# Value matmuls of the feed-forward units: 512 columns in every second step in place of 256 in every step

## The reference

```python
def ffn(hidden_states, ...):                 # twice, with the same weights
    weights = softmax over the top 2 of 4 experts, from the pooled tokens
    q, k, v = [hidden_states @ (mix of the experts' W) + b]   # B=2, T=1024, H=16, D=8
    scores = einsum('bthd,bshd->bhts', q, k) / sqrt(D)
    attn = softmax(scores, axis=-1)
    out = einsum('bhts,bshd->bthd', attn, v).reshape(B, T, C)
    return out @ Wo + bo
x = x + 0.5 * ffn(layernorm(x))
x = x + causal_attention(layernorm(x))
x = x + 0.5 * ffn(layernorm(x))
```

## Time and profile before

| | |
|---|---|
| median of three executions | 1330.35 us (1326.4 to 1460.52) |
| the profiled execution | 1325.41 us, of which the span from the first to the last instruction is 1323.7 us |
| PE busy in the span | 1180.9 us (89%) |
| DVE busy | 1073.0 us (81%) |
| ACT busy | 918.3 us (69%) |
| POOL busy | 343.3 us (26%) |
| exponentials of the units, line 761 | 1024 of 598 ns |
| row maxima, line 925 | 512 of 1217 ns |
| value matmuls, line 1228 | 3584 records |

### The profile page before, as it was taken

One profiled execution on the slowest core, in us unless ns is written; L12 is line 12 of the kernel. 1 busy time (PEld: TensorE's weight loads), 2 busy tenths in 40 slices (PEclk: granted clock), 3 DMA queues, 4 the chain that ended last, 5 costly groups with the idle time before them and its releaser, 6 DMA issues. The chain is left out here.

```text
span 1323.7 us, 33144 instructions
## 1 busy us (share of the span) xinstructions
PE 1180.9 (89%) x10992; PEld 495.5 (37%) x10992; DVE 1073.0 (81%) x1749; ACT 918.3 (69%) x1943; POOL 343.3 (26%) x777
## 2 busy tenths in 40 slices
PE   4499999999987999999989999997869999999996
PEld 3122222222244555555565555554722222222222
DVE  6899999999986677766736777666489999999996
ACT  3189999988955666666635666665328999998893
POOL 4400000002002455544424555445220000000200
PEclk9689999999997999999999999998968999999998
DMA  4711122443111000000000000000333122244312
GB/s 101 226 43 50 55 64 61 89 85 79 48 45 27 20 20 19 20 19 20 20 19 19 20 20 19 20 18 1 99 92 93 47 58 60 61 89 85 85 41 64
DMA packets 53811, 70.06 MB, mean 53 GB/s; under 512 B 21264, under 2 KB 31440, under 8 KB 53712
## 3 DMA queue, kind: packets, MB, share of 16 engines
q1 hardware_dynamic: 53712, 68.75, 20.9%
HBM read 37.79 MB, written 22.54 MB: 46 GB/s over the span
## 5 line engine op out<-in xcount | busy, mean ns | idle before, releaser
L925 DVE TENSOR_REDUCE neg_max<-ps 128x1 f32<-128x1024 f32 x512 | 591.6, 1217 | 23.2 <-PE ps L1197 21.4
L761 ACT ACTIVATE arena<-ps 128x512 f32<-128x512 f32 x1024 | 545.4, 598 | 83.0 <-PE ps L1212 70.7
L1212 PE MATMUL ps<-arena 50*128 50x512 bf16 x1024 | 322.8, 387 | 15.5 <-ACT arena L761 9.9
L1228 PE MATMUL ps<-arena 128*32 128x256 f32 (+1 forms) x3584 | 315.8, 424 | 8.7 <-ACT arena L761 3.1
L1197 PE MATMUL ps<-arena 48*128 48x512 bf16 x1024 | 297.5, 396 | 14.9 <-DVE neg_max L925 13.9
L1001 DVE TENSOR_REDUCE a_neg_max<-ps 128x1 f32<-128x129 f32 (+7 forms) x256 | 192.9, 753 | 130.8 <-PE ps L1335 130.4
L688 ACT ACTIVATE arena<-ps 128x64 f32<-128x64 f32 (+7 forms) x256 | 104.5, 408 | 172.4 <-PE ps L1349 170.3
L682 ACT ACTIVATE arena<-ps,a_neg_max 128x129 f32<-128x129 f32 (+7 forms) x256 | 189.4, 740 | 33.1 <-DVE a_neg_max L1001 32.0
L1329 PE MATMUL ps<-arena 64*128 64x321 f32 (+7 forms) x512 | 192.1, 456 | 7.6 <-ACT arena L682 5.1
L596 POOL TENSOR_SCALAR arena<-arena,a_rsum 128x128 f32<-128x128 f32 (+7 forms) x256 | 190.7, 745 | 18.3
L1331 PE MATMUL ps<-arena 64*128 64x320 f32 (+7 forms) x512 | 191.9, 456 | 0.0
(11 more groups left out here) (120 smaller groups left out, 920.3 us busy)
## 6 DMA issues: line engine op xcount, KB each, us to landing
arena<-stack_dram SPq DMA_DIRECT2D x128, 192.0 KB, 3.3
stack_dram<-arena SPq DMA_DIRECT2D x48, 256.0 KB, 3.7
o_dram<-arena SPq DMA_DIRECT2D x32, 256.0 KB, 2.1
arena<-arena SPq DMA_DIRECT2D x32, 256.0 KB, 3.6
arena<-o_dram SPq DMA_DIRECT2D x30, 256.0 KB, 4.2
arena<-max_dram SPq DMA_DIRECT2D x256, 1.0 KB
x<-in_L_attn_x SPq DMA_DIRECT2D x2, 512.0 KB, 4.8
max_dram<-max_T SPq DMA_DIRECT2D x64, 8.0 KB, 1.6
```

The lines of the kernel that those rows point to most:

```text
L761: nc.scalar.activation(probs[:, t, :], ps[:, EXP_BANK[t], :], ACT.Exp, scale=F_SCALE).then_inc(probs_ready, 1)
L925: nc.vector.tensor_reduce(neg_max[:, g, t:t + 1], ps[:, bank:bank + 2, :].rearrange("p a b -> p (a b)"), AX, ALU.max, negate=True).then_in ...
L1212: ins = nc.tensor.matmul(ps[:, bank, :], stack[rows, g, 1, kt * P:(kt + 1) * P], stack[rows, g, 0, h * HALF:(h + 1) * HALF], start=True, s ...
L1228: ins = nc.tensor.matmul(ps[row:row + 32, PV_BANK, cols], v_unit[:, g, t // 2, :], probs[:, t, cols], start=j == 0 and c0 == 0 and g % 2 == 0,
```

## The change

In steps 2, 4 and 6 no values are issued; in steps 3, 5 and 7 the whole group is, at 512 columns in one pass:

```diff
                     score_tile(g, it, kt, 1)
-                    if kt >= 2:
-                        values(g, it, kt // 2 - 1, kt % 2 * (HALF // 2), (kt % 2 + 1) * (HALF // 2))
+                    if kt >= 2 and kt % 2:
+                        values(g, it, kt // 2 - 1, 0, HALF)
                     elif kt == 0 and not first:
                         values((g - 1) % NB, it if g else it - 1, NT // 2 - 1, 0, HALF)
```

## The result

The changed kernel takes 1374.24 us (median of four executions, 1370.64 to 1380.0); the kernel before 1328.88 us (median of four, three of which are those told above). The ratio is 1.0353, with a 95% interval of 1.0321 to 1.0384: slower. It is taken without the one execution of 1460.52 us, which was in a slow state, so from 1327.4 us. Forecast were 1376 us and a range of 1358 to 1392.

The account below looks back on a forecast made before the run. The prediction took a loop of score tile, exponential, bank reuse and queued value group to bind the changed kernel: 60 units x 0.82 = 49 us on 1325.4 gives 1374 us profiled, 1376 us median, range 1358 to 1392.

Parts of the forecast that it names:

- What PE saves is worth nothing: Merging halves saves PE 0.66 us a unit, but PE already waits nearly 1 us there, so no gain by itself.
- Steps 0 to 3: From a unit's tile 0 to tile 8: 4.99 us, or 5.14 with the copy of line 751 on ACT.
- Steps 4 and 5: From tile 8 to tile 12: 0.50 + 0.65 + 1.31 = 2.46 us.
- Steps 6 and 7: Tile 12 to next tile 0: 2.88 us, as tile 15 takes tile 13's bank, one exponential more.
- The unit: Tile 0 to the next unit's tile 0: mean 10.41 us against 9.59 before, 0.82 us more.
- Four units hide it: In four units the added time replaces waits for the maxima's transfers, at about no cost; the other 60 lose 49 us.
- The sum: 1325.4 + 49 = 1374 us for the profiled execution; 1376 us for the median of new runs.
- the loop: Score tile, exponential, tile three on reusing its bank, group queued behind, next score tile: 0.82 us more a unit, chance 0.81.
- ACT idle 0.5 to 0.9 us behind each group: Sign expected in the new profile: ACT, with three tiles to read, runs dry behind each value group for 0.5 to 0.9 us.
- The first rival: Saved matmul time comes through: 1307 us, or 1326 to 1335 if ACT's slack only absorbs the gaps; together 0.11.
- DVE's floor: Eight row maxima and one transpose on DVE: 8 x 1.13 + 0.20 = 9.24, about 9.3 us under any unit making maxima.
- The clock: Rival: with PE less busy the granted clock falls to 0.80, the four groups lengthen, 1444 us; chance 0.05.

Follow-up runs that it names:

- light maxima: The changed kernel with the row maximum taken over 256 of the 1024 keys: 1363.37 us, ratio 1.0297 to the kernel before.
- the other turn of the banks: The changed kernel with score tiles taking their three banks in another order, so tile 15 waits for exponential 12, not 13: 1341.64 us, ratio 1.0114.
- the turn of the banks: The kernel before with another order of its three banks, tile 15 waiting for exponential 12, not 13: 1326.12 us, ratio 0.9995.
- the third turn: The kernel before with the short bank reuses at tiles 2 and 4, so neither tile 15 nor tile 1 waits for the exponential two back: 1321.22 us, ratio 0.996.
- two passes: The changed kernel with the group of steps 3, 5 and 7 issued as two 256-column passes, one right behind the other: 1376.71 us, ratio 1.038.
- half groups: The changed kernel with the second 256 columns of groups 0 to 2 left out of the computation: 1318.22 us, ratio 0.9937.

## Why the prediction was right

Point by point, by its own steps:

- *What PE saves is worth nothing.* Right. By the prediction's count a unit needs 0.66 us less of PE, and it takes 0.84 us more. The time from the last tile before a group to the next tile is 1.31 us in the new profile too (1125.57 to 1126.88).
- *Steps 0 to 3.* Forecast 4.99 us from tile 0 to tile 8 in a unit without the copy; 1121.88 to 1126.88 is 5.00. The small part that DVE has in it was right as well: the max tile ahead of tile 7 waits 0.27 us for DVE, and with light maxima just 0.09 of it went.
- *Steps 4 and 5.* 2.46 forecast, 2.47 measured. *Steps 6 and 7.* 2.88 forecast, 2.87 measured; with the other turn of the banks it is 2.39, so 0.48 of them is the bank of tile 15.
- *The unit.* 10.41 forecast, 10.42 measured, against 9.59 and 9.58.
- *Four units hide it.* Right: behind the first units no score tile of the new profile waits for the maxima's transfers, and those four units are no longer than their neighbours. All five waits of the earlier trace rows were over 0.6 us; the fifth, of the second feed-forward's first unit, is still there, 0.7 us. 60 x 0.82 = 49 us was the sum; the two loops grew by 47.6.
- *The sum.* 1374 us was forecast for the profiled execution, and it took 1380.0: the loops are there, and outside them 7 us that the sum did not have. 1376 us for the median came within 2 us of 1374.24, but the prediction put the median above the profiled execution, and it lies 5.8 us below it. So close a hit of the median is partly luck, in executions that spread over 9 us; the loop and its 48 us are not.
- *ACT idle 0.5 to 0.9 us behind each group.* Partly wrong: 0.81, 0.36, 0.49 and 0.33 us. The prediction counted three exponentials ahead of the gap; the timeline has four, the last one of the tile that had stopped.
- *The first rival, that saved matmul time comes through,* needed tile 8 to tile 11 in 0.95 us. It is 1.15 (1126.88 to 1128.03). Where the groups were cut to 256 columns, 0.88 us from tile to tile, the condition reads 2.26 - 0.88 = 1.38, which 1.15 meets: the loop fell below DVE's floor and the unit came down to it. That smaller pieces speak for the loop was the prediction's own step: the passage of the Trainium skill that it weighed there ("Perfetto Trace Analysis", Optimizing Scalar/DVE Operations) is on breaking up ScalarE's and VectorE's instructions, and the pieces here are TensorE's.
- *What bounds the kernel before* was told only in part. I named DVE's floor and the waits behind the whole group, and put PE's slack at about 1 us. That a loop through the banks and group 0 gives 9.44 us was not seen; it came out when the turn of the banks changed nothing there, and the third turn, which cuts it, took 0.12 us off the unit. It had no part in the forecast, since the new loop is longer than either.
- *The clock.* Right in the steady stretch, 1.00. At one place behind it did fall, see below; the chance was given to a fall everywhere.

## What to carry to other kernels

When several engines are nearly full, write down the loop through each ring of buffers: tile, reader, the tile that reuses the buffer, and everything that the in-order engine has queued behind that tile. Here three banks stood against four score tiles between two groups, so longer and fewer matmuls that saved PE 0.66 us a unit made it 0.84 longer, and the two lowest times, 1317 and 1314 us, came with shorter pieces. The place of the one short reuse in a table of banks was worth 32 us in the changed kernel and nothing in the old one, where the stop only moved from tile 15 to the next unit's tile 1.

## What the runs showed of the hardware that I had not expected

The granted clock fell in the changed kernel where PE had still less to do. The last two units of a feed-forward have no max tiles. In the profiled execution the windows of the last unit but one and the last one of the first feed-forward, and of the last one of the second, are (columns as above):

```profile
382.00:393.30 11.30, 8.95 (x48) 1.71 (x47) 6.78 (x5) 8.79 (x17) 2.92 (x4) 0.88 0.19 49
393.30:406.60 13.30, 11.95 (x48) 1.72 (x48) 10.49 (x8) 7.79 (x16) 0.00 (x0) 0.50 0.00 0
...
1350.80:1360.00 9.20, 7.12 (x48) 1.74 (x48) 7.25 (x7) 7.79 (x16) 0.00 (x0) 1.00 0.03 4
```

A granted clock of 0.50 is the level of 1.2 GHz. From its tile 0 to its last exponential the last unit took 13.3 us there and 9.1 at the same place of the second feed-forward, with the same work; before, both took 9.0 at 1.00. On PE, ahead of the fall, the timeline shows waits of 0.63, 0.55 and 0.96 us for exponentials, and then groups of 1.93 us where they were 1.07:

```profile
390.90 0.60 PE L1212 MATMUL ps<-arena 50*128 50x512 bf16 x1 [0.96 <-ACT arena L761]
391.44 1.93 PE L1228 MATMUL ps<-arena 128*32 128x512 f32 x8
```

That is 4.3 us of the 7 which the profiled execution lost outside the loops; the unit ahead of it lost 1.1 more, which counts in the loops. The other 3.1 us lie between the last exponential of the first feed-forward and the first maximum of the second, a part that takes 584.4 to 589.3 us in the twelve profiles of this case.

Two more kernels with whole groups in steps 3, 5 and 7 fell so in the last unit but one, where the max tiles have just ended: the one with two passes in the first feed-forward, and the one with light maxima in the second. It took 13.1 and 13.0 us, where it is 10.3 in the other feed-forward:

```profile
380.95:394.07 13.12, 11.19 (x77) 2.78 (x74) 8.60 (x7) 8.79 (x17) 2.93 (x4) 0.68 0.16 42
```
```profile
1320.30:1333.30 13.00, 11.07 (x54) 1.80 (x50) 8.63 (x5) 8.79 (x17) 2.54 (x2) 0.69 0.16 42
```

The kernel with half groups shows a fall in the middle of a feed-forward (told there), behind a score tile that had waited 2.0 us for the maxima's transfers.

Why the clock held in the other feed-forward with the same work stays open: in the changed kernel PE waited 0.63, 0.55 and 0.96 us there too. Whether such falls make the spread of 1370.6 to 1380.0 us isn't shown, since only the profiled execution has a timeline. The mean granted clocks speak for it. Those of the four are 0.951, 0.954, 0.958 and 0.958 at 1380.0, 1377.6, 1370.6 and 1370.9 us; with light maxima it is 0.955 in the one execution of 1374.3 us and 0.963 in the three of about 1363.
